# The last batch of a transformer tail in two staggered token halves

## The chip, the cores and the metric

One Trainium2 (trn2) chip; the kernel runs on one of its cores. The metric is device time in microseconds (us) of one execution, median of 3 runs. The core has TensorE (PE, weight loads shown apart as PEld), VectorE (DVE), ScalarE (ACT), GpSimd (POOL) and SyncE (SP), which here issues nearly all DMAs. Each engine has its own instruction stream and works through it in order; engines wait for one another on semaphores.

## The reference

Two layers act on x of 8 batches x 256 tokens x 128 features. Only the end of the second is touched by the change: attention's output product, a linear map with a weight per batch, and a feed-forward part with quantized activations and weights.

```python
def _quant_act(x):
    scale = 127.0 / jnp.clip(jnp.max(jnp.abs(x), axis=-1, keepdims=True), EPS, None)
    xq = jnp.clip(jnp.round(x * scale), -128.0, 127.0) / scale
    return xq                                   # (straight-through terms left out)
def _bitlinear(x, w):
    return jnp.einsum('bsi,oi->bso', _quant_act(x), _quant_weight(w))

x = x + attention(pooled) ...                   # y @ w_out, y: (8, 256, 1024)
c = einsum('bnh,boh->bno', x, weight[subject_id]) + bias[subject_id]
x = x + _bitlinear(gelu(_bitlinear(c, w1)), w2) # 128 -> 512 -> 128
```

## The kernel before

The first 1100 us or so are a state-space layer and a mixture of experts; they are not touched. Then comes attention with the feed-forward part, batch by batch. Four strings of tokens (`ATT_PE`, `ATT_ACT`, `ATT_DVE`, `ATT_GP`) give, for each engine, the order of pieces in one slot; `run` walks through the slots k = -4 to 8 and emits for each token the piece of batch k + shift. The pieces of the end of a batch have the shift -1: they belong to the batch whose heads were done in the slot before. So the end of batch 6 is mixed with the 16 heads of batch 7, while slot 8 holds the end of batch 7 and nothing beside it.

The end of a batch is one chain that passes from engine to engine, for both halves of 128 tokens (t = 0, 1) in one go, all in PSUM bank 7:

- `o2` (PE, L826): y times `Wo`, 16 matmuls over 8 chunks and 2 halves; each f32 matmul is two records in the trace. It waits for the eighth copy of y (`yTe`, ACT, L819).
- `x3` (DVE, L832) adds the residual; `fx` turns it (PE L838, copy ACT L843); `fc` is the product with the batch's weight (PE L849) and the bias (DVE L855).
- `fq` (DVE, L860 to L872): largest magnitude of each token, its scale and inverse, then a multiply and an add of 1.5 * 2^23 per half (L867), which rounds, and two passes that take the constant off, with the bound 127 (L871), and apply the bound -128 (L872), which writes bf16.
- `fqturn` and its copy (PE L886, ACT L891), `fu` (PE L901), gelu (`fg`, ACT L905, two instructions of 128x512); `fq2` is the same quantization on 256x512; `fq2turn` (PE L924), its copy (DVE L929), `fd` (PE L935), `fo` (DVE L943), and one store of 128 KB that SP issues.

`warm:n` (L569) is padding: n products of constants in bank 5, two records each, for the last batch alone. ACT's exp and gelu lie in different tables, and a load stands ahead of the first function of the other set (L905 and L764).

Attention itself: `score` (L747), `tt` (DVE L756), `prob` (exp, ACT L764), `inv` (DVE L770), `norm` (POOL L777, four instructions for a pair of heads), `turn` (PE L785) with a copy on DVE or ACT (L794, L792), `values` (L811), `yturned` (L819).

## Time and profile before

| | us |
|---|---|
| median of 3 runs (lowest, highest) | 1392.04 (1388.57, 1392.33) |
| the profiled execution, its own time | 1390.29 |
| its span, first to last instruction | 1388.5 |
| PE busy, of the span | 1280.7 (92%) |
| DVE / ACT / POOL busy | 1156.7 / 1006.7 / 1106.3 |
| mean granted TensorE clock | 0.985 |
| issue to landing of the eight result stores of 128 KB, lowest / median / highest | 1.8 / 1.9 / 2.7 |

Busy times are sums over stages with different limits. From about 1103 us on, each batch of attention takes 39.86 us; the heads of the last batch end at 1367 us, and what follows is the chain above alone. Starts in the rows are us from the span's start.

### The profile page before, as it was taken

The page shows a single profiled execution, that of the slowest core. Times are in us where ns is not written, and L with a number is a line of the kernel's source. Part 1 is how long each engine was busy: PE and PEld are TensorE (multiplying, and loading weights), DVE is VectorE, ACT ScalarE, POOL GpSimd, SP SyncE. Part 2 cuts the span into 40 slices and gives each one's busy share as a digit, 9 for nine tenths or more (in the row PEclk, how much of TensorE's full clock was granted, in tenths as well). Part 3 has the DMA queues.
Part 4 walks back from the last instruction along what each step waited for, and adds up shares of the span by engine and source line. Part 5 has one row for each costly group of instructions (what it writes and reads, how often), then busy time and mean ns, then how long its engine had stood idle before and what let it go on. Part 6 is the DMA issues. An engine that isn't in the chain of part 4 may idle for free.

```text
span 1388.5 us, 20349 instructions
## 1 busy us (share of the span) xinstructions
PE 1280.7 (92%) x5604; PEld 726.6 (52%) x5613; DVE 1156.7 (83%) x1710; ACT 1006.7 (73%) x2377; POOL 1106.3 (80%) x676
## 2 busy tenths in 40 slices
PE   6598998998998989989989999899999999999997
PEld 2243443343343334334343356689986666766665
DVE  7899999999999999999999989765545466665664
ACT  4778878878878878878878888433326787887783
POOL 7789999999999999999999998034435766856662
PEclk9799999999999999999999999999999999999999
DMA  4645254255164154164244372413221000000000
GB/s 145 274 183 196 109 211 199 106 213 209 65 248 199 70 242 183 69 255 183 108 204 184 130 238 78 145 39 93 80 58 35 9 20 15 22 17 17 9 9 8
DMA packets 48979, 169.29 MB, mean 122 GB/s; under 512 B 15704, under 2 KB 33436, under 8 KB 40716
## 3 DMA queue, kind: packets, MB, share of 16 engines
q1 hardware_dynamic: 46636, 163.78, 30.9%
q0 software_dynamic: 2272, 4.66, 1.5%
q8 instruction: 33, 0.54, 0.2%
q14 instruction: 38, 0.31, 0.1%
HBM read 160.75 MB, written 7.67 MB: 121 GB/s over the span
## 4 chain that ended last, share of the span: by engine, by line
PE 47%; DVE 24%; ACT 14%; issue 11%; DMA 1%; POOL 1%; DVEq 0%; ACTq 0%; POOLq 0%; SPq 0%
DVE h L1255 13%; ACT banks L1220 10%; PE banks L1290 7%; DVE h L1236 5%; PE banks L402 5%; PE banks L747 4%; PE banks L811 3%; PE banks L785 3%; PE banks L411 3%; PE banks L687 2%; PE banks L826 2%; PE banks L704 2%; PE banks L724 2%; PE banks L1141 2%; PE banks L1307 2%
## 5 line engine op out<-in xcount | busy, mean ns | idle before, releaser
L1261 POOL TENSOR_TENSOR h<-h,Cb 128x1024 f32<-128x1024 f32 (+1 forms) x180 | 584.4, 3273 | 24.6 <-DVE h L1255 13.3
L1255 DVE TENSOR_TENSOR_SCAN h<-banks,h 128x1024 f32<-128x1024 f32 x256 | 573.8, 2277 | 15.3 <-ACT banks L1220 14.9
L1220 ACT ACTIVATE banks<-dt,A_cur 128x255 f32<-128x255 f32 x1024 | 422.2, 461 | 86.8 <-DVE h L1255 84.7
L1290 PE MATMUL banks<-h,ident 128*128 128x512 f32 x1024 | 468.8, 597 | 4.4 <-POOL h L1261 2.6
L1290 PEld LDWEIGHTS banks<-h,ident 128*128 128x128 f32 x1024 | 189.9, 190 | 246.5 <-issue 225.3
L1236 DVE TENSOR_TENSOR h<-Bb,banks 128x1024 f32<-128x1024 f32 (+1 forms) x131 | 204.6, 1567 | 3.2 <-ACT banks L1204 3.2
L1242 POOL TENSOR_TENSOR h<-Bb,u 128x1024 f32<-128x1024 f32 x80 | 188.4, 2366 | 0.1
L777 POOL TENSOR_SCALAR h<-h 128x128 f32<-128x128 f32 (+1 forms) x128 | 97.2, 774 | 61.8 <-DVE h L770 61.8
L777 POOL TENSOR_SCALAR Cb<-Cb,h 128x128 f32<-128x128 f32 (+1 forms) x128 | 101.1, 806 | 34.9 <-DVE h L770 34.7
L1115 PE MATMUL banks<-xn,wF 128*128 128x512 f32 x256 | 114.9, 601 | 7.4 <-ACT xn L1107 7.4
L1115 PEld LDWEIGHTS banks<-xn,wF 128*128 128x128 f32 x256 | 48.7, 191 | 72.1 <-issue 61.4
L381 POOL COPY Bb<-Bb 128x1 int32 x39 | 10.5, 268 | 83.2 <-DVE Bb L1663 45.4
L402 PE MATMUL banks<-Cb 128*128 128x128 f32 x624 | 76.1, 275 | 0.2 <-ACT Cb L450 0.2
L402 PEld LDWEIGHTS banks<-Cb 128*128 128x128 f32 x624 | 72.7, 192 | 0.4 <-ACT Cb L450 0.4
L756 DVE CUSTOM_DVE_ANT_0 h<-banks,Bb 128x128 f32<-128x128 f32 (+1 forms) x128 | 38.5, 352 | 26.2 <-PE banks L747 26.1
L747 PE MATMUL banks<-h 64*128 64x128 f32 (+1 forms) x512 | 59.3, 350 | 0.9
L811 PE MATMUL banks<-Bb,h 128*64 128x256 f32 (+1 forms) x512 | 55.7, 338 | 1.3 <-ACT Bb L792 0.8
L487 DVE TENSOR_TENSOR Cb<-Cb,banks 128x512 f32<-128x512 f32 x39 | 26.8, 688 | 36.0 <-PE banks L402 36.0
L764 ACT ACTIVATE Cb<-Cb,h 128x128 f32<-128x128 f32 (+1 forms) x128 | 56.7, 449 | 0.1
L764 ACT ACTIVATE h<-h 128x128 f32<-128x128 f32 (+1 forms) x128 | 56.6, 452 | 0.0
L553 POOL DMA_INDIRECT xm<-by_expert,Bb x32 | 31.5, 985 | 24.1 <-DMA by_expert<-Cb 15.8
L383 POOL DMA_INDIRECT Cb<-by_token,Bb x39 | 38.6, 989 | 14.9 <-POOL Bb L381 14.9
(296 smaller groups left out, 2041.5 us busy)
## 6 DMA issues: line engine op xcount, KB each, us to landing
Bb<-scrX SPq DMA_DIRECT2D x32, 2048.0 KB, 8.0
Cb<-scrX SPq DMA_DIRECT2D x32, 2048.0 KB, 9.5
h<-in_L_ffn_w SPq DMA_DIRECT2D x2, 2048.0 KB, 8.5
by_expert<-Cb SPq DMA_DIRECT2D x39, 64.0 KB, 1.5
h<-in_conv_w SPq DMA_DIRECT2D x4, 512.0 KB, 4.0
scr<-h SPq DMA_DIRECT2D x3, 640.0 KB, 15.0
wF<-scr SPq DMA_DIRECT2D x3, 512.0 KB
dt<-in_pmask SPq DMA_DIRECT2D x4, 257.0 KB, 2.7
```

The lines of the kernel that those rows point to most:

```text
L402: m = e.matmul(bank(2 * w + q)[:, c * P:(c + 1) * P], w_now[q][w][:, c * P:(c + 1) * P], xgT[k], start=True, stop=True)
L747: m = e.matmul(bank(o)[:, lo:lo + n], qT[r:r + HS, p, jc * P:(jc + 1) * P], kT[r:r + HS, p, 0:n], start=True, stop=True)
L764: m = e.activation(Pr[h % 8][:, lo:lo + n], Pr[h % 8][:, lo:lo + n], ACT.Exp, bias=negm[:, jc, h:h + 1], scale=-1.0, accum_out=sums[:, jc, ...
L777: m = e.tensor_scalar(Pr[h % 8][:, lo:lo + n], Pr[h % 8][:, lo:lo + n], inv[:, jc, h:h + 1], None, ALU.mult)
L811: m = e.matmul(bank(4, S)[o * HS:(o + 1) * HS, q0:q0 + n], V[:, kc, h * HS:(h + 1) * HS], PT[h % 4][:, 2 * P * kc:2 * P * kc + n], start=( ...
L1115: m = e.matmul(ps_F[half][:].rearrange("p (b l) -> p b l", b=2), wF[:, FC_TAP + k * 2 * P + half * P:FC_TAP + k * 2 * P + (half + 1) * P], ...
L1220: m = e.activation(ps_dA[c % 2][:, g, half, 1:S], dts[q][:, half, i * S + 1:(i + 1) * S], ACT.Exp, scale=A_cur[q][:, s:s + 1])
L1236: e.tensor_tensor(h[i][:, rows(cs), :, :], both(Bb[i], cs), u_rows(ps_u, cs), ALU.mult).then_inc(sem("mulv"), len(cs))
L1242: e.tensor_tensor(h[i][:, rows(cs), :, :], both(Bb[i], cs), u_rows(us[q][:, :, i * S:(i + 1) * S], cs), ALU.mult).then_inc(sem("mulp"), le ...
L1255: e.tensor_tensor_scan(chunk(i, c), ps_dA_flat[c % 2], chunk(i, c), 0.0, ALU.mult, ALU.add).then_inc(sem("scan"), 1)
L1261: e.tensor_tensor(h[i][:, rows(cs), :, :], h[i][:, rows(cs), :, :], both(Cb[i], cs), ALU.mult).then_inc(sem("hC"), len(cs))
L1290: m = e.matmul(bank(5), ident[:], h_flat[i][:, s * HALVES * S:(s + 1) * HALVES * S], start=(s == 0), stop=(s == NS - 1))
```

## The change

All pieces of slot 8 with the shift -1 leave the common loop. For the last batch their place is taken by new functions that treat one half of the tokens each, in an order of their own (`ENDING`). Half 0 works in bank 7, half 1 in bank 6, each with its own semaphore steps. The copy before `fd` moves from DVE to ACT. `gelus` loads the gelu table right behind the last copy of y. The result is stored in two DMAs of 64 KB.

In every batch, `q_clip` loses its second instruction: the first writes bf16 directly, with the bound 127 and no bound at -128 (the scale makes no value go below -127).

In slot 8 of the loop `warm:l8` and `warm:l23` are gone; `warm:l2` stays in `ATT_PE` (its piece has the shift 0, so it isn't skipped), and `ENDING` has `warm:2`, `warm:8` and `warm:5`.

```diff
@@ -367,8 +367,11 @@
                     mask(b + 3)
                 if b + 1 < B:
                     conditioned(b + 1)
-                result(b)
-            e.wait_ge(sem("out"), 16 * B + 16)
+                    result(b)
+            for t in range(2):
+                e.wait_ge(sem("f_o"), 2 * B + 1 + t)
+                dma(out_tok[:, END * 2 + t:END * 2 + t + 1, :], fo[:, t:t + 1, :], "out")
+            e.wait_ge(sem("out"), 16 * B + 32)
 
 
         def tail_gpsimd(e):
@@ -868,12 +871,11 @@
 
         def q_clip(m, tmp_t, dst, name):
             m.sync()
-            m(m.e.tensor_scalar(tmp_t, tmp_t, -ROUND, 127.0, ALU.add, ALU.min)); m.sync()
-            m.e.tensor_scalar(dst, tmp_t, -128.0, None, ALU.max).then_inc(sem(name), 1)
+            m.e.tensor_scalar(dst, tmp_t, -ROUND, 127.0, ALU.add, ALU.min).then_inc(sem(name), 1)
 
         def dve_fq(e, b):
             e.wait_ge(sem("f_c"), b + 1)
-            m = Chain(e, "du", chained[0] + b * 14)
+            m = Chain(e, "du", chained[0] + b * 12)
             q_scales(m, fc, 1)
             q_round(m, fc, ft)
             q_clip(m, ft, fq, "f_q")
@@ -906,7 +908,7 @@
 
         def dve_fq2(e, b, step):
             e.wait_ge(sem("f_g"), 2 * b + 2)
-            m = Chain(e, "du", chained[0] + b * 14 + 7)
+            m = Chain(e, "du", chained[0] + b * 12 + 6)
             if step == 0:
                 q_scales(m, fg, 0)
             elif step == 1:
@@ -944,6 +946,105 @@
                                        scalar=fr[:, 0, t:t + 1], in1=fst[:, t, :], op0=ALU.mult, op1=ALU.add
                                        ).then_inc(sem("f_o"), 1)
 
+
+        def half(x, t):
+            return x[:, t * P:(t + 1) * P]
+
+        def pe_o2_end(e, part):
+            t = 1 if part else 0
+            e.wait_ge(sem("yTe"), 8 * B)
+            e.wait_ge(sem("f_o"), 2 * B)
+            for c in ((range(8), range(4), range(4, 8))[part]):
+                m = e.matmul(bank(7 - t, P), yT[:, c, t * P:(t + 1) * P], Wo[:, c, :], start=(c == 0), stop=(c == 7))
+            if part != 1:
+                m.then_inc(sem("o2"), 1)
+
+        def dve_x3_end(e, t):
+            e.wait_ge(sem("o2"), B + t)
+            e.tensor_tensor(fst[:, t, :], xt[:, 2 * END + t, :], bank(7 - t, P), ALU.add).then_inc(sem("x3"), 1)
+
+        def pe_fx_end(e, t):
+            e.wait_ge(sem("x3"), B + t)
+            e.transpose(bank(7 - t, P), fst[:, t, :], ident[:]).then_inc(sem("fx_ps"), 1)
+
+        def act_fx_end(e, t):
+            e.wait_ge(sem("fx_ps"), B + t)
+            e.activation(half(fx3T, t), bank(7 - t, P), ACT.Copy).then_inc(sem("fx"), 1)
+
+        def pe_fc_end(e, t):
+            e.wait_ge(sem("fx"), B + t)
+            e.wait_ge(sem("cw"), 32 * B)
+            e.matmul(bank(7 - t, P), half(fx3T, t), fcw, start=True, stop=True).then_inc(sem("fc_ps"), 1)
+
+        def dve_fc_end(e, t):
+            e.wait_ge(sem("fc_ps"), B + t)
+            e.wait_ge(sem("cw"), 32 * B)
+            e.tensor_tensor(fc[:, t, :], bank(7 - t, P), fcb, ALU.add).then_inc(sem("f_c"), 1)
+
+        def levels_end(m, t, src, dst, row, tmp_t, name):
+            m(m.e.tensor_reduce(fr[:, 2, t:t + 1], src[:, t, :], AX_X, ALU.max, apply_absolute_value=True)); m.sync()
+            m(m.e.tensor_scalar(fr[:, 2, t:t + 1], fr[:, 2, t:t + 1], Q_EPS, 1.0 / 127.0, ALU.max, ALU.mult)); m.sync()
+            m(m.e.reciprocal(fr[:, 3, t:t + 1], fr[:, 2, t:t + 1]))
+            m(m.e.tensor_scalar(fr[:, row, t:t + 1], fr[:, 2, t:t + 1], fsm[:, 10 + (row != 1):11 + (row != 1)], None,
+                                ALU.mult)); m.sync()
+            m(m.e.tensor_scalar(tmp_t[:, t, :], src[:, t, :], fr[:, 3, t:t + 1], ROUND, ALU.mult, ALU.add)); m.sync()
+            m.e.tensor_scalar(dst[:, t, :], tmp_t[:, t, :], -ROUND, 127.0, ALU.add, ALU.min).then_inc(sem(name), 1)
+
+        def dve_fq_end(e, t):
+            e.wait_ge(sem("f_c"), B + t)
+            levels_end(Chain(e, "du", chained[0] + END * 12 + t * 5), t, fc, fq, 1, ft, "f_q")
+
+        def pe_fqturn_end(e, t):
+            e.wait_ge(sem("f_q"), B + t)
+            e.transpose(half(bank(7 - t).bitcast(BF16), 0), fq[:, t, :], idb).then_inc(sem("fqT_ps"), 1)
+
+        def act_fqturned_end(e, t):
+            e.wait_ge(sem("fqT_ps"), B + t)
+            e.activation(half(fqT, t), half(bank(7 - t).bitcast(BF16), 0), ACT.Copy).then_inc(sem("fqT"), 1)
+
+        def pe_fu_end(e, t):
+            e.wait_ge(sem("fqT"), B + t)
+            e.matmul(bank(7 - t), half(fqT, t), f1q, start=True, stop=True).then_inc(sem("fu_ps"), 1)
+
+        def act_gelus_end(e):
+            e.preload_act_table_set("gelu_and_others")
+
+        def act_fg_end(e, t):
+            act_fg(e, END, t)
+
+        def dve_fq2_end(e, t):
+            e.wait_ge(sem("f_g"), 2 * B - 1 + t)
+            levels_end(Chain(e, "du", chained[0] + END * 12 + 10 + t * 5), t, fg, fq2, 0, ft2, "f_q2")
+
...
+        def dve_fo_end(e, t):
+            e.wait_ge(sem("fd_ps"), B + t)
+            e.wait_ge(sem("out"), 16 * B)
+            e.scalar_tensor_tensor(out=fo[:, t, :], in0=bank(7 - t, P), scalar=fr[:, 0, t:t + 1], in1=fst[:, t, :],
+                                   op0=ALU.mult, op1=ALU.add).then_inc(sem("f_o"), 1)
+
+        ENDS = dict(
+            gp=dict(),
+            pe=dict(warm=lambda e, n: turn_over(e, 5, n), o2=pe_o2_end, fx=pe_fx_end,
+                    fc=pe_fc_end, fqturn=pe_fqturn_end, fu=pe_fu_end, fq2turn=pe_fq2turn_end, fd=pe_fd_end),
+            act=dict(fx=act_fx_end, fqturned=act_fqturned_end, fg=act_fg_end, fq2turned=act_fq2turned_end),
+            dve=dict(x3=dve_x3_end, fc=dve_fc_end, fq=dve_fq_end, fq2=dve_fq2_end, fo=dve_fo_end))
 
         PIECES = dict(
             gp=dict(gather=(4, gp_gather), norm=(0, gp_norm)),
@@ -964,11 +1065,19 @@
                 for token in order.split():
                     name, _, arg = token.partition(":")
                     shift, fn = PIECES[engine][name]
+                    if k == B and shift < 0:
+                        continue
                     shift += {"l": -1, "n": 1}.get(arg[:1], 0)
                     if not isinstance(k, int) or 0 <= k + shift < B:
                         fn(e, k + shift, *((int(arg.lstrip("ln")),) if arg else ()))
             for k in range(-4, B + 1):
                 slot(k)
+            for token in ENDING[engine].split():
+                name, _, arg = token.partition(":")
+                if name == "gelus":
+                    act_gelus_end(e)
+                else:
+                    ENDS[engine][name](e, int(arg))
 
 
         block = ctx.enter_context(nc.Block())
@@ -1944,12 +2053,19 @@
 
 
 X2T_AFTER = (3, 4, 5)
+END = B - 1
+ENDING = dict(
+    gp="",
+    pe="""o2:0 o2:1 fx:0 o2:2 fc:0 fx:1 fc:1 warm:2 fqturn:0 fu:0 fqturn:1 fu:1 warm:8
+       fq2turn:0 fd:0 warm:5 fq2turn:1 fd:1""",
+    act="gelus fx:0 fx:1 fqturned:0 fg:0 fqturned:1 fg:1 fq2turned:0 fq2turned:1",
+    dve="x3:0 x3:1 fc:0 fq:0 fc:1 fq:1 fq2:0 fq2:1 fo:0 fo:1")
...
 ATT_PE = """
 score:4 turn:2 o2 hold:12 pturn score:5 turn:3 values:0 fx turn:4 warm:l2 pool score:6 fc turn:5 values:1 turn:6 q:0
-score:7 turn:7 k:0 values:2 warm:l8 turn:8 turn:9 fqturn q:1 fu:0 score:n0 values:3 fu:1 k:1 turn:10 turn:11 fold
-heat:32 x2t q:2 warm:5 turn:12 score:n1 values:4 q:3 k:2 at warm:l23 turn:13 score:n2 values:5 v:0 fq2turn k:3 S
+score:7 turn:7 k:0 values:2 turn:8 turn:9 fqturn q:1 fu:0 score:n0 values:3 fu:1 k:1 turn:10 turn:11 fold
+heat:32 x2t q:2 warm:5 turn:12 score:n1 values:4 q:3 k:2 at turn:13 score:n2 values:5 v:0 fq2turn k:3 S
...
```

PE, from the padding ahead of the output product to the turn of the quantized values. Before (L826 output product, L838 `fx`, L849 `fc`, L569 padding, L886 `fqturn`):

```order
L569 MATMUL banks<-ident,center_w 128x128 x3
L826 MATMUL banks<-h,Cb 128x128 x16
L838 MATMUL banks<-ident,yz 128x128 x2
L569 MATMUL banks<-ident,center_w 128x128 x2
L849 MATMUL banks<-xs,u 128x128 x2
L569 MATMUL banks<-ident,center_w 128x128 x8
L886 MATMUL banks<-Bb,dt 128x128 x2
```

The same place now (L958 output product, L968 `fx`, L977 `fc`, L572 padding, L999 `fqturn`):

```order
L572 MATMUL banks<-ident,center_w 128x128 x5
L958 MATMUL banks<-h,Cb 128x128 x12
L968 MATMUL banks<-ident,yz 128x128
L958 MATMUL banks<-h,Cb 128x128 x4
L977 MATMUL banks<-xs,u 128x128
L968 MATMUL banks<-ident,yz 128x128
L977 MATMUL banks<-xs,u 128x128
L572 MATMUL banks<-ident,center_w 128x128 x2
L999 MATMUL banks<-Bb,dt 128x128
```

The turn of half 0 has moved in between the chunks of half 1, and the two padding products that stood behind `fx` now stand with the other three ahead of the output product.

PE, from `fu` to its last instruction. Before (L901 `fu`, L924 `fq2turn`, L935 `fd`):

```order
L901 MATMUL banks<-xs,dt 128x512 x2
L569 MATMUL banks<-ident,center_w 128x128 x23
L924 MATMUL banks<-Bb,h 128x128 x8
L935 MATMUL banks<-xs,Bb 128x128 x8
L88 UNCONDITIONAL_BRANCH
```

Now (L1007 `fu`, L1022 `fq2turn`, L1033 `fd`):

```order
L1007 MATMUL banks<-xs,dt 128x512
L999 MATMUL banks<-Bb,dt 128x128
L1007 MATMUL banks<-xs,dt 128x512
L572 MATMUL banks<-ident,center_w 128x128 x8
L1022 MATMUL banks<-Bb,h 128x128 x4
L1033 MATMUL banks<-xs,Bb 128x128 x4
L572 MATMUL banks<-ident,center_w 128x128 x5
L1022 MATMUL banks<-Bb,h 128x128 x4
L1033 MATMUL banks<-xs,Bb 128x128 x4
```

The padding is in two lots, and each lot stands ahead of the turn of one half.

ACT, from the last two copies of y to its end. Before (L819 copy of y, L843 `fx`, L891 `fqturned`, L905 gelu):

```order
L819 ACTIVATE Cb<-banks 128x256 x2
L843 ACTIVATE u<-banks 128x256
L891 ACTIVATE dt<-banks 128x256
L905 ACT_TABLE_LOAD
L905 ACTIVATE h<-banks,yz 128x512 x2
```

Now (L822 copy of y, L972 `fx`, L1003 `fqturned`, L907 gelu, L1027 the copy ahead of `fd`):

```order
L822 ACTIVATE Cb<-banks 128x256 x2
L1010 ACT_TABLE_LOAD
L972 ACTIVATE u<-banks 128x128 x2
L1003 ACTIVATE dt<-banks 128x128
L907 ACTIVATE h<-banks,yz 128x512
L1003 ACTIVATE dt<-banks 128x128
L907 ACTIVATE h<-banks,yz 128x512
L1027 ACTIVATE Bb<-banks 128x512 x2
```

The load has moved ahead of both `fx` copies, and ACT has two more instructions of 128x512. On DVE the new order is `x3:0 x3:1`, then bias and quantization of half 0, the same of half 1, then both of the second quantization, then `fo:0 fo:1`.

## Rows read from the trace of the kernel before

**Rows 1.** Busy time by window, one steady batch: us, busy us (instructions), clock, DMA share, GB/s.

```profile
1222.54:1262.40 39.86, 39.61 (x289) 27.41 (x290) 26.00 (x116) 31.86 (x104) 24.96 (x33) 1.00 0.05 14
```

**Rows 2.** The chain that ended last, in the last heads: start, us, what.

```profile
1358.53 1.48 issue
...
1361.48 2.39 POOL Cb L777 x3
```

**Rows 3.** Timeline from 1366 us on: start, us, engine line op, xcount, idle before.

```profile
1366.63 0.94 PE L569 MATMUL banks<-ident,center_w 128*128 128x128 f32 x6
...
1367.40 3.74 PE L826 MATMUL banks<-h,Cb 128*128 128x128 f32 x32
...
1372.56 0.71 PE L849 MATMUL banks<-xs,u 128*128 128x128 f32 x4
...
1374.23 0.17 DVE L861 TENSOR_SCALAR yz<-yz 128x2 f32<-128x2 f32 x1
...
1374.76 0.48 DVE L867 TENSOR_SCALAR dt<-u,yz 128x128 f32<-128x128 f32 x2
...
1376.28 0.38 ACT L891 ACTIVATE dt<-banks 128x256 bf16<-128x256 bf16 x1 [3.76 <-PE banks L886]
1376.68 1.28 ACT L905 ACT_TABLE_LOAD   x1
...
1376.94 0.38 PE L901 MATMUL banks<-xs,dt 128*128 128x512 bf16 x1 [0.70 <-ACT dt L891]
...
1383.52 0.62 PE L924 MATMUL banks<-Bb,h 128*128 128x128 bf16 x8 [1.07 <-DVE h L872]
...
1385.59 0.61 DVE L943 SCALAR_TENSOR_TENSOR Bb<-banks,yz 128x128 f32<-128x128 f32 x2 [0.71 <-PE banks L935]
```

**Rows 4.** DVE groups by shape, 1371 to 1389 us: xcount, busy us, mean ns, idle before.

```profile
L860 DVE TENSOR_REDUCE yz<-h 128x2 f32<-128x1024 f32 x1 | 1.2, 1220 | 3.4 <-ACT h L905 3.4
L867 DVE TENSOR_SCALAR h<-h,yz 128x512 f32<-128x512 f32 x2 | 0.9, 483 | 0.0
L872 DVE TENSOR_SCALAR h<-h 128x1024 bf16<-128x1024 f32 x1 | 0.7, 695 | 0.0
...
L943 DVE SCALAR_TENSOR_TENSOR Bb<-banks,yz 128x128 f32<-128x128 f32 x2 | 0.6, 348 | 0.7 <-PE banks L935 0.7
...
L855 DVE TENSOR_TENSOR u<-banks,xs 128x256 f32<-128x256 f32 x1 | 0.4, 425 | 1.7 <-PE banks L849 1.7
...
L860 DVE TENSOR_REDUCE yz<-u 128x2 f32<-128x256 f32 x1 | 0.4, 420 | 0.0
...
L872 DVE TENSOR_SCALAR dt<-dt 128x256 bf16<-128x256 f32 x1 | 0.3, 294 | 0.0
```

**Rows 5.** ACT groups by shape, 900 to 1389 us.

```profile
L455 ACT ACTIVATE Cb<-banks 128x512 f32<-128x512 f32 x39 | 23.3, 597 | 23.8 <-PE banks L402 23.8
...
L450 ACT ACTIVATE Cb<-banks 128x128 f32<-128x128 f32 x39 | 10.7, 278 | 54.1 <-PE banks L394 54.1
...
L905 ACT ACTIVATE h<-banks,yz 128x512 f32<-128x512 f32 x16 | 10.1, 684 | 0.1
```

**Rows 6.** DVE's timeline at 1360 us.

```profile
1360.59 0.74 DVE L872 TENSOR_SCALAR h<-h 128x1024 bf16<-128x1024 f32 x1
```

**Rows 7.** POOL groups: first instruction of the last `norm`; two like it, 1355.5 to 1358.6 us.

```profile
L777 POOL TENSOR_SCALAR Cb<-Cb,h 128x128 f32<-128x128 f32 x1 | 1.4, 1421 | 1.5 <-DVE h L770 1.5
...
L777 POOL TENSOR_SCALAR Cb<-Cb,h 128x128 f32<-128x128 f32 x2 | 1.2, 602 | 0.0
```

**Rows 8.** Windows in the state-space layer and in the old tail, columns as in rows 1.

```profile
160.00:162.00 2.00, 0.05 (x2) 0.03 (x1) 2.00 (x3) 1.97 (x4) 2.00 (x2) 1.00 0.45 188
162.00:163.00 1.00, 1.00 (x2) 0.48 (x3) 0.93 (x1) 1.00 (x4) 1.00 (x1) 0.55 0.00 0
...
1374.00:1377.00 3.00, 1.41 (x13) 1.21 (x13) 1.72 (x8) 0.71 (x2) 0.00 (x0) 1.00 0.00 0
```

**Rows 9.** PE groups, 907 to 911 us, where the granted clock was 0.50.

```profile
L569 PE MATMUL banks<-ident,center_w 128*128 128x128 f32 x10 | 2.3, 421 | 0.0
```

More of the change, by code:

```diff
@@ new lines, in pe_fq2turn_end, with act_fq2turned_end, pe_fd_end @@
+        def pe_fq2turn_end(e, t):
+            e.wait_ge(sem("f_q2"), B + t)
+            for c in range(FC):
+                m = e.transpose(half(bank(7 - t).bitcast(BF16), c), fq2[:, t, c * P:(c + 1) * P], idb)
+            m.then_inc(sem("fq2T_ps"), 1)
+        def act_fq2turned_end(e, t):
+            e.wait_ge(sem("fq2T_ps"), B + t)
+            e.activation(fq2T[:, t, :, :], fold(bank(7 - t).bitcast(BF16)[:, 0:FC * P], FC), ACT.Copy
+                         ).then_inc(sem("fq2T"), 1)
+        def pe_fd_end(e, t):
+            e.wait_ge(sem("fq2T"), B + t)
+            for c in range(FC):
+                m = e.matmul(bank(7 - t, P), fq2T[:, t, c, :], f2q[:, c, :], start=(c == 0), stop=(c == 3))
+            m.then_inc(sem("fd_ps"), 1)
```

## The prediction

> **What bounds the kernel now.** I first read the busy windows of the attention stage. A steady batch takes 39.86 us, and PE is busy for 39.61 of them, DVE for 26.00 and ACT for 31.86 [rows 1]: seven of the eight batches are bound by PE. The reader is to see there that a DVE instruction less per batch can give at most the 0.25 us in which PE isn't busy. The chain of waits then shows where this ends: in the heads of the last batch it runs through POOL's `norm`, and there is a wait of 1.48 us in it, in which POOL stands until ACT has done the last exps [rows 2]. Last comes the timeline behind the last `values`. From 1367.40 us, when the output product starts, to 1386.20, when the second `fo` is done, every step waits for the one before it [rows 3]: 18.80 us, on engines of which one works at a time. The store and its end take the 2.29 us up to the span's end. The change works on these 18.80 us, so durations and hand-overs count here, and no engine's share does.
>
> **Output product to `fc`.** I count from the start of the output product as 0. Its 32 records take 3.74 us, 0.112 us from start to start [rows 3]. Half 0 is done after 16 of them, at 1.96; the addition takes 0.29 (425 ns for 256 elements less 128 times 1.04 ns, the slope between the two reductions of 420 and 1220 ns) [rows 4]. `x3:0` is thus done at 2.29, `fx:0` fits in between the chunks of half 1 (it delays them by 0.14), and its copy on ACT takes 278 ns [rows 5]. The product ends at 3.88, `x3:1` at 4.21, and `fc:0` on PE at 4.16, with the 0.3 us of a single f32 product there [rows 3]. From here DVE has no pause: it is what sets the end of the first quantization.
>
> **First quantization.** One half: reduction 0.29, the three operations on the scales 0.53 from the start of L861 to that of L867 [rows 3], L867 0.28 (483 ns less 384 times 0.52), and the one pass that is left 0.23 (294 ns less 128 times 0.52 ns, where 0.52 is the slope up to 695 ns) [rows 4]; with hand-overs of 0.04 this is 1.41 us. With the bias before it (0.29 and 0.04) half 0 is done at 5.97 and half 1 at 7.73. Before, the turned values of both halves were ready for ACT 8.88 after the start (L891 at 1376.28 [rows 3]); those of half 1 now are at 8.05, after a turn of 0.22. So the second set of small operations has eaten most of what the stagger gives here: 0.83 us are left.
>
> **The way through PE and ACT.** From 5.97 on half 0 goes on beside DVE's work for half 1: turn 0.22 and 0.06 to get there, copy 0.28, `fu` 0.38, gelu 0.68 (684 ns, [rows 5]), 1.77 with the hand-overs, so the gelu is done at 7.74, when DVE is free too. This needs the table to be there. Before, ACT's load ran from 1376.68 to 1377.96, and `fu` was done by about 1377.15, so the load cost 0.8 us of waiting [rows 3]. Now it runs while PE computes the output product, which takes 3.74 us against 1.28 for the load; nothing else is asked of ACT there. If that cover were gone, the 0.6 us that the load would overhang come back.
>
> [...]
>
> **Second quantization.** One half of 512 elements: 0.69 for the reduction, 0.53, L867 0.48, last pass 0.43 [rows 4], 2.20 with hand-overs. DVE does both without a pause: 9.98 and 12.21. Before, PE got the result at 16.12 (L924 at 1383.52 [rows 3]). This step carries most of the gain: 0.8 from the table, 0.7 from the pass that is dropped, and the rest from half 0's way through PE and ACT, which is hidden now.
>
> **The end, and the padding.** `fu:1` is issued at 8.6. Behind it stand 16 records of padding, 1.8 us, up to 10.40; `fq2turn:0` was ready at 10.04 and waits. It takes 0.39 for 4 of the 8 products of 0.62 [rows 3], the copy on ACT 0.60 (597 ns, [rows 5]; before it was on DVE, 0.69 for both halves), `fd:0` 0.39: done at 11.88. Then 10 records of padding hold PE up to 12.84, while half 1 is ready for it at 12.27. So here the change adds a wait of 0.57 us, with `fq2turn:1`, `fd:1`, DVE's `fo:1` and SP's second store queued behind it. Turn 0.39, copy 0.60, `fd:1` 0.39, `fo:1` 0.35 and four hand-overs give 14.70. Against 18.80 this is 4.10 us less. SP has no other transfer by then, and the first store (ready at 12.6) is 2 us ahead. The second is 64 KB instead of 128 KB; its price isn't in the trace. A store of 128 KB took 1.8 to 2.7 us to land, so it lies between 0.9 lost (median to highest) and 0.4 gained (if half the moving goes); I take 0.15 gained, since nothing but size differs from the median one.
>
> **Ahead of the output product.** The padding there was 6 records and is 10 now, since `warm:l2` runs one place earlier than it did. The product started right behind the padding (6 records from 1366.63 on, then 1367.40 [rows 3]), so 4 x 0.112 = 0.45 us are lost. In the last heads L872 goes away beside the last `norm`. POOL's first instruction there took 1421 ns, from 1360.06 to 1361.48 [rows 7], where the same shape took 602 in the `norm` before it, and DVE's L872 stood from 1360.59 to 1361.33 beside it [rows 6]. The 0.82 us extra lie beside 0.50 us of L871 and 0.74 us of L872; by its share L872's part is 0.5. The path from there to the output product is POOL, turn, `values`, and moves up with it. [...] The two other effects of the dropped pass come to nothing: the first quantization of batch 6, which stands ahead of an `inv` of the last heads, lets POOL start 0.3 earlier, but that runs into the wait of 1.48 [rows 2]; in the seven PE-bound batches I take 0, bounds 0 and 7 x 0.25 = 1.75.
>
> [...]
>
> **Sum.** 4.10 + 0.15 - 0.45 + 0.50 = 4.3 us. The profiled execution took 1390.29, hence 1386.0. The median of the three runs shown is 1.75 above it, the lowest 1.72 below; the mean of all four times is 1390.8. A median of the changed kernel is as likely to lie high as low, so I forecast 1386.5.
>
> **Rivals.** *Padding at half clock.* The new order leaves PE with little to do from 5.8 to 8.5: two turns and two products, with pauses of up to 1.1 us. [...] In the old tail it held 1.00 through 3 us in which PE was busy for 1.41 [rows 8]; the new pauses have about as much work between them. If it falls, the padding costs twice as much, 0.23 us a record instead of 0.112 (10 took 2.3 us at half clock [rows 9]): the first lot ends at 12.2, the second at 16.2, `fo:1` at 18.35. Of the 4.3 us 3.65 are gone: 1389.6 against the profiled execution.
>
> *The PE-bound batches gain too.* If PE's 0.25 us are waits for DVE, the seven batches give up to 1.75 more: 1384.2. For it: PE's weight loads for L811 sometimes wait for a DVE copy. Against: the matmuls before them are still running then.
>
> *A collision in each batch, the side of slower.* With L872 gone DVE reaches its next passes 0.74 us earlier, and they may fall beside a `norm` that had been free; one costs POOL 0.82 us as above. If PE waited for it in each of the seven batches, 5.7 us come on top: 1391.7, slower than before. It decides from the sixth batch that pays. Against it: POOL is idle for 14.9 of 39.86 us, and PE isn't waiting for it [rows 1].
>
> **Chances.** The sum 60%, the PE-bound batches 15%, the half clock 18%, the collisions 7%. A measurement of this kernel tells about 0.3%, 4.2 us, from no change, and the sum lies right at that line: of its 60 I give 38 to faster and 22 to within. With 15 for the PE-bound batches faster has 53; within has 22, 16 of the half clock and 5 of the collisions, 43; slower by over 0.3% is left with 4. The range takes in the half clock below and the gain in the batches above: 1383.2 to 1390.0.
>
> **What would show it.** Right: one table load between the last copy of y and `fx:0`; DVE without a pause from `x3:1` to the end of the second quantization, some 8.3 us; `fo:1` 14.7 us after the start of the output product; PE's padding right up to `fq2turn:1`; 10 records of padding ahead of the product; the last `norm` in about 3.3 us instead of 3.80; steady batches of 39.86. Wrong: a granted clock under 1.00 between `fqturn:0` and `fd:1`; steady batches shorter or longer by over 0.1 us; DVE pauses of over 0.2 us ahead of `fq2:0`, which would mean that half 0's way through PE and ACT is longer than the 1.77 us.

## The result and the profile after

The changed kernel takes 1385.96 us (median of 8, 1385.39 to 1390.67) where the kernel before takes 1390.15 in the same comparison (median of 8, 1388.57 to 1392.33): ratio 0.9973, 95% interval 0.9961 to 0.9985. By the medians that is 4.2 us faster, 0.5 us under the forecast of 1386.5; by the ratio it is 3.8 us, with an interval from 2.1 to 5.4. The interval leaves out a ratio of 1, so the kernel is faster; but 0.27% is a little under the 0.3% that the prediction took as the least that can be told from no change. Its profiled execution took 1387.39 us, with a span of 1385.6 and a mean granted clock of 0.986.

That execution is only 2.9 us under the profiled one of before. The first record of the first output product in the attention stage shows why. It is at 1102.79 us before:

```profile
1102.79 0.61 PE L826 MATMUL banks<-h,Cb 128*128 128x128 f32 x4
```

and at 1104.60 after:

```profile
1104.60 0.61 PE L829 MATMUL banks<-h,Cb 128*128 128x128 f32 x4
```

All that comes ahead of it is state-space work that the change doesn't touch, and it took 1.81 us longer in this execution. In the traces of e1 to e4 below, which ran on one chip, this start lies between 1101.30 and 1104.32, so it moves by some 3 us from one execution to the next. I therefore measure each trace from this record on, in three distances: *heads*, up to the start of the last output product; *ending*, from there to the end of the last `fo`; *store*, from there to the end of the span (the span is given to 0.1 us, so this last one is good to 0.05).

| us | before | after | difference | predicted |
|---|---|---|---|---|
| heads | 264.61 | 264.60 | -0.01 | -0.05 (0.45 lost, 0.50 gained) |
| ending | 18.80 | 14.41 | -4.39 | -4.10 |
| store | 2.30 | 1.99 | -0.31 | -0.15 |
| together | 285.71 | 281.00 | -4.71 | -4.3 |

The steady batch, the window that answers to [rows 1] (columns as there):

```profile
1224.35:1264.21 39.86, 39.60 (x289) 27.41 (x290) 25.09 (x114) 31.84 (x104) 24.52 (x33) 1.00 0.05 14
```

DVE has 0.91 us less to do, the batch is as long as it was. The ending, the timeline that answers to [rows 3]; the output product starts at 1369.20:

```profile
1367.98 1.38 PE L572 MATMUL banks<-ident,center_w 128*128 128x128 f32 x10
...
1368.49 1.28 ACT L1010 ACT_TABLE_LOAD   x1
1369.20 2.84 PE L958 MATMUL banks<-h,Cb 128*128 128x128 f32 x24
1371.19 0.29 DVE L964 TENSOR_TENSOR yz<-Cb,banks 128x128 f32<-128x128 f32 x1 [3.38 <-PE banks L958]
...
1374.77 0.23 DVE L991 TENSOR_SCALAR dt<-dt 128x128 bf16<-128x128 f32 x1
1374.92 0.28 DVE L982 TENSOR_TENSOR u<-banks,xs 128x128 f32<-128x128 f32 x1
...
1375.65 0.10 PEld L1007 LDWEIGHTS banks<-xs,dt 128*128 128x128 bf16 x1 [0.50 <-ACT dt L1003]
...
1376.09 0.69 ACT L907 ACTIVATE h<-banks,yz 128x512 f32<-128x512 f32 x1 [0.48 <-remote]
1376.37 0.23 DVE L991 TENSOR_SCALAR dt<-dt 128x128 bf16<-128x128 f32 x1
...
1376.81 0.69 DVE L985 TENSOR_REDUCE yz<-h 128x1 f32<-128x512 f32 x1 [0.21 <-ACT h L907]
...
1377.48 1.95 PE L572 MATMUL banks<-ident,center_w 128*128 128x128 f32 x16
...
1379.27 0.39 PE L1022 MATMUL banks<-Bb,h 128*128 128x128 bf16 x4
...
1380.58 1.33 PE L572 MATMUL banks<-ident,center_w 128*128 128x128 f32 x10
1380.62 0.43 DVE L991 TENSOR_SCALAR h<-h 128x512 bf16<-128x512 f32 x1
...
1381.75 0.39 PE L1022 MATMUL banks<-Bb,h 128*128 128x128 bf16 x4
1382.17 0.60 ACT L1027 ACTIVATE Bb<-banks 128x512 bf16<-128x512 bf16 x1 [1.88 <-PE banks L1022]
1382.82 0.40 PE L1033 MATMUL banks<-xs,Bb 128*128 128x128 bf16 x4 [0.69 <-ACT Bb L1027]
1383.26 0.35 DVE L1039 SCALAR_TENSOR_TENSOR Bb<-banks,yz 128x128 f32<-128x128 f32 x1 [1.95 <-PE banks L1033]
```

The reader is to see three things. The table load lies beside padding and output product. From 1373.08 (`x3:1`) to 1381.05 DVE stops once, for 0.21 us. And `fq2turn:1` (L1022, the second time) has its input at 1381.05 and its first product at 1381.75, because padding is ahead of it. One record is missing: the product of `fu:0` (L1007), of which only the weight load at 1375.65 was recorded, so the gelu behind it shows "remote" as its releaser. POOL's first instruction of the last `norm`, the group that answers to [rows 7]:

```profile
L780 POOL TENSOR_SCALAR Cb<-Cb,h 128x128 f32<-128x128 f32 x1 | 1.0, 972 | 1.9 <-DVE h L773 1.9
```

972 ns instead of 1421. Windows (columns as in rows 1) of the long pause of PE in the last heads, and of the thin and the full stretch of the ending:

```profile
1359.90:1362.30 2.40, 0.01 (x2) 0.00 (x0) 1.72 (x6) 2.29 (x10) 0.54 (x2) 1.00 0.00 0
1362.30:1366.00 3.70, 2.95 (x27) 2.03 (x29) 1.68 (x4) 1.03 (x3) 2.90 (x4) 1.00 0.00 0
1374.00:1377.00 3.00, 1.40 (x8) 1.03 (x9) 2.52 (x13) 1.11 (x4) 0.00 (x0) 1.00 0.00 0
1377.00:1379.00 2.00, 1.75 (x15) 1.72 (x16) 1.86 (x7) 0.89 (x2) 0.00 (x0) 1.00 0.00 0
```

The granted clock is 1.00 in all of them. In the third window PE was busy for more than the 1.40 us shown, since the missing `fu:0` lies in it; e11 below has its record, 0.39 us, which makes 1.79. The experiments show that in both places the clock is less certain than it looks.

### The profile page after: what moved, and what is told of

Read it like the earlier page. It is cut to its first block, busy times and chain, and to the rows that moved or that the text cites. A ratio compares the mean times of both kernels' runs of the same rounds, so it can differ in the third digit from the quotient of the medians.

```text
span 1385.6 us, 20287 instructions
## 1 busy us (share of the span) xinstructions
PE 1276.5 (92%) x5572; PEld 722.1 (52%) x5581; DVE 1150.2 (83%) x1705; ACT 1008.1 (73%) x2381; POOL 1102.0 (80%) x676
## 4 chain that ended last, share of the span: by engine, by line
PE 47%; DVE 23%; ACT 14%; issue 11%; DMA 2%; POOL 1%; DVEq 0%; ACTq 0%; SPq 0%; POOLq 0%
DVE h L1364 13%; ACT banks L1329 10%; PE banks L1399 7%; DVE h L1345 5%; PE banks L405 5%; PE banks L750 4%; PE banks L814 3%; PE banks L788 3%; PE banks L414 3%; PE banks L690 2%; PE banks L707 2%; PE banks L727 2%; PE banks L1416 2%; PE banks L1250 2%; PE banks L829 2%
## 5 line engine op out<-in xcount | busy, mean ns | idle before, releaser
L780 POOL TENSOR_SCALAR Cb<-Cb,h 128x128 f32<-128x128 f32 (+1 forms) x128 | 98.0, 782 | 37.1 <-DVE h L773 37.0
L453 ACT ACTIVATE Cb<-banks 128x128 f32<-128x128 f32 x39 | 10.8, 277 | 54.8 <-PE banks L397 54.8
```

The lines of the kernel that those rows point to most:

```text
L780: m = e.tensor_scalar(Pr[h % 8][:, lo:lo + n], Pr[h % 8][:, lo:lo + n], inv[:, jc, h:h + 1], None, ALU.mult)
```

## The experiments

Ratios are against the kernel before, run in the same comparison. e1 to e4 ran on one chip, e5 to e8 on a second and e9 to e12 on a third (the kernel before took 1390.51, 1406.11 and 1405.66 us there). The distances are of each one's trace. A steady batch takes 39.86 us on all three chips, so the distances can be compared; medians can't, ratios with care.

| us | heads | ending | store | median | ratio (95%) |
|---|---|---|---|---|---|
| before | 264.61 | 18.80 | 2.30 | 1390.15 | |
| after | 264.60 | 14.41 | 1.99 | 1385.96 | 0.9973 (0.9961 to 0.9985) |
| e1 one-pass rounding alone | 264.66 | 17.73 | 2.29 | 1390.41 | 0.9996 (0.9987 to 1.0005) |
| e2 two-pass rounding | 265.03 | 16.26 | 2.01 | 1388.16 | 0.9981 (0.9972 to 0.9990) |
| e3 no early load | 264.62 | 16.58 | 2.00 | 1387.72 | 0.9978 (0.9969 to 0.9987) |
| e4 halves in step | 264.58 | 20.54 | 1.93 | 1392.29 | 1.0016 (1.0006 to 1.0025) |
| e5 no padding in the ending | 265.21 | 14.20 | 2.03 | 1401.14 | 0.9965 (0.9953 to 0.9978) |
| e6 lots 2 and 3 doubled | 264.60 | 17.31 | 1.96 | 1404.38 | 0.9985 (0.9975 to 0.9994) |
| e7 no `warm:l2` | 264.14 | 14.41 | 1.99 | 1400.50 | 0.9961 (0.9949 to 0.9974) |
| e8 one store | 265.22 | 14.41 | 2.31 | 1401.85 | 0.9966 (0.9955 to 0.9978) |
| e9 as e3, pauses filled | 264.60 | 15.01 | 2.02 | one run | |
| e10 as e2, pauses filled | 265.05 | 14.96 | 2.00 | one run | |
| e11 leaner ending | 264.76 | 13.61 | 2.02 | 1399.39 | 0.9948 (0.9928 to 0.9968) |
| e12 as e11, last heads padded | 264.14 | 13.60 | 2.00 | 1399.91 | 0.9956 (0.9939 to 0.9973) |

Among the 17 executions of the kernel before that stand beside e9 to e12, one took 3347.41 us and is in no ratio, and one took 1416.12 us at a mean clock of 0.934 and is in them. The ratio of e11 is lower than its medians give (1399.39 to 1405.66, 0.9955).

**e1, the rounding alone.** The kernel before with

```diff
-            m(m.e.tensor_scalar(tmp_t, tmp_t, -ROUND, 127.0, ALU.add, ALU.min)); m.sync()
-            m.e.tensor_scalar(dst, tmp_t, -128.0, None, ALU.max).then_inc(sem(name), 1)
+            m.e.tensor_scalar(dst, tmp_t, -ROUND, 127.0, ALU.add, ALU.min).then_inc(sem(name), 1)
```

> The kernel before with the one-pass rounding alone (last batch in its old form, old padding). My theory: PE bounds the steady batches, so they stay at 39.86 us; the last norm on POOL falls from 3.80 to about 3.3 us; in the last batch the two dropped passes take 0.29 and 0.70 us off the 18.80 us from the start of the last output product to the second fo, which comes to 17.8. In all about -1.5 us. Rival (PE waits for DVE in the batches): the batches come to 39.6 and the time falls by up to 1.75 more, -3.2. Rival (collisions with POOL): batches longer than 39.96 and a time above the kernel before.

Measured: batches of 39.86 us, last `norm` 3.35 us, ending 17.73. The ending and the batches came as expected, and both rivals fall. The 0.45 us of the `norm` don't show in the heads, though (264.66 and not 264.15), and the timed runs show 0.1 us, within an interval from 1.8 us faster to 0.7 slower. In this trace the kernel gained 1.0 us from the first output product on, where 1.5 was expected. What took the 0.5 back is told below e8.

**e2, two passes again in the changed kernel.** The edit above undone, and in the ending

```diff
-            m.e.tensor_scalar(dst[:, t, :], tmp_t[:, t, :], -ROUND, 127.0, ALU.add, ALU.min).then_inc(sem(name), 1)
+            m(m.e.tensor_scalar(tmp_t[:, t, :], tmp_t[:, t, :], -ROUND, 127.0, ALU.add, ALU.min)); m.sync()
+            m.e.tensor_scalar(dst[:, t, :], tmp_t[:, t, :], -128.0, None, ALU.max).then_inc(sem(name), 1)
```

> The changed kernel with the rounding in two passes again, in the batches and in both halves of the ending. My theory: DVE sets the end through both quantizations, and per half a second pass costs about 0.23 + 0.04 us (first) and 0.43 + 0.04 us (second), so four of them lengthen the ending's 14.41 us by 1.5 to 15.9, less what the padding held anyway (0.65 us ahead of fq2turn:1: PE's padding would be done before DVE, so only about 0.9 to 1.0 net, 15.3 to 15.4). The last norm goes back to about 3.80. In all +1.4 us. Rival (the clip is hidden, hand-overs set the ending): the ending stays under 14.8.

The `norm` is back at 3.80 and the heads are 0.43 longer, as expected. The ending is longer than expected by 0.9 us, 16.26. Windows of this trace (columns as in rows 1), and the second lot of padding in its timeline:

```profile
1372.00:1375.00 3.00, 1.13 (x6) 0.38 (x5) 2.72 (x12) 1.24 (x3) 0.00 (x0) 1.00 0.00 0
1376.00:1378.00 2.00, 2.00 (x11) 1.94 (x10) 1.86 (x7) 0.02 (x1) 0.00 (x0) 0.50 0.00 0
```

```profile
1375.14 3.07 PE L572 MATMUL banks<-ident,center_w 128*128 128x128 f32 x16
```

The clock has fallen to 0.50 after a stretch in which PE was busy for 1.13 of 3 us, and the 16 records take 3.07 instead of 1.95 us.

**e3, no early load.**

```diff
-    act="gelus fx:0 fx:1 fqturned:0 fg:0 fqturned:1 fg:1 fq2turned:0 fq2turned:1",
+    act="fx:0 fx:1 fqturned:0 fg:0 fqturned:1 fg:1 fq2turned:0 fq2turned:1",
```

> The changed kernel without the early load of the gelu table: the load of 1.28 us then stands between the copy fqturned:0 and gelu 0. My theory: the copy ends 6.4 us after the start of the output product, fu:0 at 6.7 hides 0.3 of it, the load ends at about 7.7 and gelu 0 at 8.4 instead of 7.58; DVE pauses for about 1.0 us ahead of fq2:0 instead of 0.2, and the padding's 0.65 us of hold takes the rest: fo:1 at about 14.6 to 14.7. Copies behind the load (fqturned:1) wait too, so gelu 1 comes at about 9.1, which DVE does not need before 10.4. In all +0.2 to +0.8. [...]

The ending is 16.58, over the expected 14.7. The timeline of this trace shows what the load took:

```profile
1373.44 0.28 ACT L1003 ACTIVATE dt<-banks 128x128 bf16<-128x128 bf16 x1 [1.26 <-PE banks L999]
...
1373.74 1.28 ACT L907 ACT_TABLE_LOAD   x1
...
1375.03 0.69 ACT L907 ACTIVATE h<-banks,yz 128x512 f32<-128x512 f32 x1
...
1375.76 0.69 DVE L985 TENSOR_REDUCE yz<-h 128x1 f32<-128x512 f32 x1 [1.03 <-ACT h L907]
...
1376.17 3.35 PE L572 MATMUL banks<-ident,center_w 128*128 128x128 f32 x16
```

The load takes 1.28 us; it starts 0.02 us behind the copy, the gelu starts 0.01 us behind the load, and it is done at 8.40 us from the start of the output product, as expected. The rest is the clock again, 0.50 from 1377 to 1379.

**e4, the halves in step.** The waits of half 0 are raised to both halves, nothing else:

```diff
         def pe_fqturn_end(e, t):
-            e.wait_ge(sem("f_q"), B + t)
+            e.wait_ge(sem("f_q"), B + 1)
         def pe_fq2turn_end(e, t):
-            e.wait_ge(sem("f_q2"), B + t)
+            e.wait_ge(sem("f_q2"), B + 1)
         def dve_fq2_end(e, t):
-            e.wait_ge(sem("f_g"), 2 * B - 1 + t)
+            e.wait_ge(sem("f_g"), 2 * B)
```

> The changed kernel with the two halves in step instead of staggered: fqturn and fq2turn of half 0 wait for the quantization of both halves, fq2 of half 0 for both gelus. All instructions are the same. My theory: the stagger hides half 0's way through PE and ACT beside DVE's work. fqturn:0 then starts at 7.4 instead of 5.9, the gelus are done at about 9.2 and 9.9 and the second quantization starts at 9.9 instead of 7.6: 2.3 us later; it ends at 14.2; both halves are then turned, copied and multiplied one behind the other, fo:1 at about 17.2 to 17.7, 2.8 to 3.3 us later than the 14.41. Rival (small halves and not the overlap give the gain): fo:1 under 15.5.

The ending is 20.54, 6.13 us longer, and the kernel is slower than the one before. The second quantization ends at 14.90 instead of 11.85, which is 3.05 later (expected: 2.3). The timeline shows the 0.75 that were not expected, and the larger part of the other 3.1 us:

```profile
1376.31 0.69 ACT L907 ACTIVATE h<-banks,yz 128x512 f32<-128x512 f32 x1 [0.48 <-PE banks L1007]
...
1376.89 0.27 ACT L1003 ACTIVATE dt<-banks 128x128 bf16<-128x128 bf16 x1
...
1384.10 2.36 PE L572 MATMUL banks<-ident,center_w 128*128 128x128 f32 x10
...
1386.26 0.63 PE L1022 MATMUL banks<-Bb,h 128*128 128x128 bf16 x4
```

In ACT's order `fqturned:1` stands behind `fg:0`. Its input was there at 1376.33, but it started at 1376.89, beside the end of the gelu; so the second gelu was done at 10.6 instead of the expected 9.9, and DVE waits for both. And I had overlooked that the third lot of padding stands between `fd:0` and `fq2turn:1`: in step both halves are ready ahead of it, and it took all of its time, at half clock (0.55 from 1384 to 1386), 2.2 us up to the turn of half 1.

So e4 measures more than the overlap. Less those 2.2 us the ending would be about 18.4 us (an estimate), about 4.0 over the staggered one, of which 0.75 are ACT's order. That is still more than the 17.73 of e1, which has whole halves and the same rounding. Halves alone gain nothing; the overlap carries the change.

**e5, no padding in the ending.**

```diff
-    ... fc:1 warm:2 fqturn:0 fu:0 fqturn:1 fu:1 warm:8 fq2turn:0 fd:0 warm:5 fq2turn:1 fd:1
+    ... fc:1 fqturn:0 fu:0 fqturn:1 fu:1 fq2turn:0 fd:0 fq2turn:1 fd:1
```

> The changed kernel without the three lots of padding products in the ending (2, 8 and 5). My theory: the second lot of 16 records does not hold fq2turn:0 much, the third of 10 holds fq2turn:1 by 0.65 us, so fo:1 comes 0.65 us earlier, at 13.75 after the start of the output product, if the granted clock stays at 1.00. Rival (the padding keeps the clock): it falls below 1.00 between fu:1 and fd:1, the eight products of fd:1 and the turns cost twice as much (0.6 us more) and fo:1 comes at 14.3 or later.

14.20, between the two. The clock did fall, and it stayed down to the last product:

```profile
1392.00:1394.00 2.00, 0.62 (x2) 0.19 (x2) 1.66 (x7) 1.36 (x3) 0.00 (x0) 1.00 0.00 0
1395.00:1399.00 4.00, 2.33 (x16) 1.27 (x15) 2.13 (x8) 1.19 (x2) 0.00 (x0) 0.50 0.06 16
```

The turn and `fd` of half 1 took 0.61 us each instead of 0.39 and 0.40, 0.43 together; of the 0.65 us that PE isn't held any more, 0.22 are left, and 0.21 were measured.

**e6, more padding.** `warm:8` to `warm:16`, `warm:5` to `warm:10`.

> The changed kernel with the second lot of padding doubled (16 turn-overs, 32 records) and the third too (10, 20 records). A record takes 0.112 us. My theory: PE is held by what is queued ahead: the second lot ends 1.79 us later, at 12.0 instead of 10.2 after the start of the output product, fq2turn:0 (ready at 10.0) waits for it, then fd:0 and 2.24 us of padding up to about 15.8, then 1.85 us to fo:1, 17.6 to 17.8: 3.3 us later. The rival (padding of no price, since PE is idle there) says 14.4.

17.31, 2.90 later, with the clock at 1.00: a little under my 17.6, and the rival falls. PE's padding is on the path here, where it is longer than its pause.

**e7, without `warm:l2` in `ATT_PE`.**

> The changed kernel without the 4 padding records ahead of the output product that were moved there (in the batches before they go as well, for the last batch alone they are issued). My theory: PE goes from the last values through 6 instead of 10 records, and the last output product starts 0.45 us earlier, from first to last output product 264.0 us instead of 264.44. Rival (yTe, the last copy of y, is what the product waits for): no difference, 264.44.

264.14 instead of 264.60: the four records cost 0.46 us.

**e8, one store.** `result(END)` in place of the two DMAs.

> The changed kernel with one store of 128 KB after both fo instead of two of 64 KB. My theory: only the size of the last store matters; from the end of fo:1 to the end of the span 1.99 us with two stores, 2.29 with one (the value of the kernel before), +0.3. Rival (two stores cost the queue a second issue and the number of stores matters, not their size): the same or shorter than 1.99.

2.31 instead of 1.99: the size of the last store counts, 0.32 us for 64 KB.

*The heads of e1, e5 and e8.* They are 0.5 to 0.6 us longer than those of kernels with the same heads (e7 for e1, the changed kernel for e5 and e8). Windows of e8 (columns as in rows 1), at the pause that PE makes there:

```profile
1374.00:1376.00 2.00, 0.11 (x1) 0.14 (x2) 1.36 (x5) 1.75 (x8) 0.59 (x1) 1.00 0.00 0
1376.00:1379.00 3.00, 3.00 (x21) 2.06 (x21) 0.43 (x2) 0.88 (x2) 2.77 (x4) 0.54 0.00 0
```

The clock fell behind the pause; in e6 and e7, with the same pause and the same work, it stayed at 1.00. So it differs between executions of the same instructions. But the kernel has a part in it too: the pause ends with the turn of head 13, and the timelines of the kernel before and of the changed one show it longer now:

```profile
1360.54 0.52 PE L785 MATMUL banks<-ident,Cb 128*128 128x128 f32 x3 [2.08 <-ACT Bb L792]
```

```profile
1362.33 0.52 PE L788 MATMUL banks<-ident,Cb 128*128 128x128 f32 x3 [2.42 <-ACT Bb L795]
```

The pause is 2.07 or 2.08 us in the three traces with two passes (before, e2, e10) and 2.40 to 2.42 in the ten that have one pass and leave the pause unfilled. The clock fell in four of these ten (e1, e5, e8 and e11 below) and in none of the three. That is too few to tell whether the longer pause brings the fall, or whether it happens to the kernel before as well.

**e9 and e10, price of load and rounding without that of the clock.** e3 and e2 with padding in PE's pauses, e9:

```diff
-    ... fqturn:0 fu:0 fqturn:1 fu:1 warm:8 ...
+    ... fqturn:0 warm:1 fu:0 warm:2 fqturn:1 warm:4 fu:1 warm:8 ...
```

and e10 in the same way with `warm:1`, `warm:3`, `warm:1`.

> The changed kernel without the early table load, with padding products in PE's pauses (2 records ahead of fu:0, 4 ahead of fqturn:1, 8 ahead of fu:1), so that the granted clock stays at 1.00. It separates the price of the load from that of the clock, which fell in e3 (0.73 in 1376 to 1377 us, then 0.50, 16 records of padding in 3.35 us instead of 1.95; tail 16.58 us). My theory: e3's +2.17 us are about 0.95 of load (gelu 0 is done 0.8 us later, then a PE that is still held by its third lot of padding) and 1.2 of half clock. Tail here 15.2 to 15.5 us, granted clock 1.00 throughout. Rival: the load costs it all and the clock nothing, tail 16.5.

> The changed kernel with the rounding in two passes, and padding in PE's pauses (2 records ahead of fu:0, 6 ahead of fqturn:1, 2 ahead of fu:1). The clock fell in e2 too (0.87 in 1375 to 1376 us, then 0.50; tail 16.26 us). My theory: with the clock at 1.00 DVE is the bound, done with fq2:1 13.05 us after the start of the output product as in e2, and PE is there at once: fo:1 at 15.0 instead of 14.41, so four passes are worth only about 0.6 net in the ending, and the other 1.25 us of e2 are the clock. Rival: DVE alone explains e2, tail 16.2 again.

e9 ends at 15.01, a little under the expected 15.2, and e10 at 14.96, as expected; the clock is at 1.00 throughout both endings. The window of e9 in which e3 had lost its clock, and the same padding:

```profile
1389.00:1392.00 3.00, 2.83 (x24) 2.57 (x24) 1.83 (x7) 2.02 (x4) 0.00 (x0) 1.00 0.00 0
```

```profile
1390.62 1.95 PE L572 MATMUL banks<-ident,center_w 128*128 128x128 f32 x16
```

So the early load is worth 0.60 us, the one-pass rounding 0.55, and half the clock cost 1.57 us in e3 (16.58 less 15.01) and 1.30 in e2 (16.26 less 14.96), more than what was tested in either. The load would have cost more but for the padding: the first gelu is done 0.83 us later in e9 than in the changed kernel, where the second lot had held `fq2turn:0` for 0.24. Filling the pauses cost nothing that shows; in e9 `fu:0` and `fu:1` start 0.05 and 0.06 us behind their copies.

All this rests on one trace of each kernel. By the ratios e2 is only 0.0008 (1.1 us) and e3 0.0005 (0.7 us) behind the changed kernel, where the traces say 2.3 and 2.2; the intervals are too wide to decide. Whether the clock falls in every execution of e2 and e3, or only in some as in the last heads, is not shown.

**e11 and e12, a version from the findings.** No `warm:l2`, no third lot, the last copy on DVE; e12 has `warm:9` ahead of `turn:13` in `ATT_PE` as well.

```diff
-       fq2turn:0 fd:0 warm:5 fq2turn:1 fd:1""",
-    act="gelus fx:0 fx:1 fqturned:0 fg:0 fqturned:1 fg:1 fq2turned:0 fq2turned:1",
-    dve="x3:0 x3:1 fc:0 fq:0 fc:1 fq:1 fq2:0 fq2:1 fo:0 fo:1")
+       fq2turn:0 fd:0 fq2turn:1 fd:1""",
+    act="gelus fx:0 fx:1 fqturned:0 fg:0 fqturned:1 fg:1 fq2turned:0",
+    dve="x3:0 x3:1 fc:0 fq:0 fc:1 fq:1 fq2:0 fq2:1 fo:0 fq2turned:1 fo:1")
```

> The changed kernel without the 4 padding records ahead of the output product, without the third lot of padding (10 records between fd:0 and fq2turn:1), and with the last copy of turned values on DVE, which is idle by then, instead of ACT; the first two lots of padding stay. My theory: the first two lots keep the clock at 1.00 through the ending (as in the changed kernel), the 0.65 us of hold go, and the DVE copy of 512 elements takes about 0.4 us instead of 0.60. From first to last output product 264.14 (264.75 where the clock falls in the last heads), tail 13.5 to 13.6 instead of 14.41. In all -1.3 us against the changed kernel, -5.5 against the kernel before, 0.9960. Rival (the clock falls after the second lot as it did in e5): tail 14.0 or more.

> The kernel of e11 with 18 more records of padding in PE's pause of 2.4 us in the last heads (between the values of heads 8 and 9 and the turn of head 13, at 1359.9 to 1362.3 us in the changed kernel). In e1, e5 and e8 the granted clock fell to 0.50 there for about 3 us, in the others not, and where it fell the last output product came 0.5 to 0.6 us later. My theory: with the pause filled (2.0 us of 2.4) the clock stays at 1.00 there in every execution, from first to last output product 264.14; the median moves by at most 0.3 us against e11, since only a part of the executions had the fall. Rival: the padding holds the turn of head 13, which is on the path of the last heads, and the distance grows to 264.5 or more.

Both end in 13.6 us, with the copy on DVE in 0.43 (e12's timeline):

```profile
1394.30 0.40 PE L1022 MATMUL banks<-Bb,h 128*128 128x128 bf16 x4 [0.36 <-DVE h L991]
...
1394.73 0.43 DVE L1032 COPY Bb<-banks 128x512 bf16<-128x512 bf16 x1 [0.23 <-PE banks L1022]
...
1395.65 0.35 DVE L1043 SCALAR_TENSOR_TENSOR Bb<-banks,yz 128x128 f32<-128x128 f32 x1 [0.49 <-PE banks L1037]
```

In the last heads of e11 the clock fell, in those of e12, with their pause filled, it stayed, and the output product started 0.62 us earlier. First e11, then e12:

```profile
1376.00:1380.00 4.00, 3.87 (x25) 2.92 (x25) 1.41 (x4) 0.87 (x2) 3.00 (x4) 0.57 0.00 0
```

```profile
1374.00:1380.00 6.00, 5.08 (x49) 3.88 (x48) 2.98 (x7) 3.20 (x11) 3.35 (x4) 1.00 0.01 3
```

e12 takes 279.74 us from the first output product to the end of the span, against 281.00 for the changed kernel and 285.71 for the one before: the expected 1.3 us. The timed runs show both faster than the kernel before; between e11, e12 and the changed kernel the intervals overlap, so that these 1.3 us, and whatever the padded heads give, rest on the traces alone; and as the clock stayed up there in six of ten traces without that padding, one trace doesn't show that it was the padding that kept it.

## Why the prediction held, step by step

**What bounds it.** Right. The batches stayed at 39.86 us in every trace, with one pass or two, and the 4.71 us came from the ending, as [rows 3] had said.

**Output product to `fc`, first quantization.** `x3:0` started at 1.99 (said: 1.96), half 0's levels were done at 5.80 (5.97), half 1's at 7.40 (7.73). I had put a hand-over of 0.04 us behind each last pass; in the trace the next operation starts 0.08 us before the pass ends (1374.77 and 0.23 to 1374.92).

**The way through PE and ACT.** 1.78 us (said: 1.77). But since half 1's levels came 0.33 earlier and this way didn't, DVE now waits for the gelu, 0.21 us. The prediction had named a pause of over 0.2 as a sign of a longer way; it was a sign of faster levels. The table load was hidden; its worth, 0.60, is 0.2 under my 0.8, which was for the old order. That it equals the 0.6 that I gave for a missing cover is luck: the gelu came 0.83 later, and the padding took 0.24 of that. The load follows the copy at once, 0.02 us behind it here and in e3, 0.01 in e9, and takes 1.28 us in each. Nor is there a wait behind it: in e3 the load ends at 1375.02, and the gelu starts at 1375.03.

**The end and the padding.** The second quantization was done at 11.85 (12.21), PE was held for about 0.65 us (0.57), `fo:1` was done at 14.41 (14.70). The gain of 4.39 is the predicted 4.10 and these 0.29. I had split it in part by the old order, with 0.7 for the dropped pass of the second quantization; in the new order both passes together give 0.55 (e10), since PE's padding takes back what DVE saves on half 1. Taken out one at a time, the load is worth 0.60, the rounding 0.55 and the overlap about 4.0; against them stand the small operations done twice and 0.80 us that e11 gets back from the third lot and the last copy on ACT.

**The store.** 0.31 gained, confirmed by e8. I had taken 0.15, with bounds of 0.4 gained and 0.9 lost; from the median to the highest landing it is 0.8 (1.9 to 2.7).

**Ahead of the output product.** 0.46 lost (said: 0.45; e7), 0.45 gained in the `norm` (said: 0.5; the heads of e2 are 0.43 longer). POOL's first instruction was still 0.37 us over its 602 ns, beside 0.50 us of DVE's single pass. Before, it was 0.82 over, beside 0.50 of L871 and 0.74 of L872. My 0.5 was an estimate that split the 0.82 by these shares; it leaves 0.33 for one pass of 0.50, and 0.37 were measured. In both traces the instruction is longer where DVE's passes lie beside it; what lengthens it isn't shown. The other effect, on the `inv` of the last heads, came to nothing as said: POOL's wait ahead of this `norm` grew from 1.5 to 1.9 us, and the `norm` started no earlier.

**The rival of the half clock.** It named the right danger, and its price was wrong. The changed kernel keeps the clock through its ending in its own trace and in those of e6, e7 and e8. In e2 to e5, with less work or longer pauses there, it fell, but each of them has a single trace. The price was 1.3 to 1.6 us and not 3.65, because the clock was back for the third lot in e2 and e3 (10 records in 1.33 us); I had let it stay at half to the end. What the prediction missed is the pause in the last heads: a fall there cost 0.5 to 0.6 us in four traces, and the dropped pass made that pause 0.34 us longer.

**The other rivals.** Neither was seen: no batch gained, none had a collision.

**What was luck.** The trace says 4.71 us and the sum said 4.3, by terms that each came out within 0.3 us. That the median lies within 0.5 us of 1386.5 says less: the part ahead of the change moves by 3 us from one execution to the next, and the 1386.5 had in it a mean of four times of the kernel before.

**What stays open.** Why the state-space part differs by up to 3 us between executions of the same code. One of the eight timed runs of the changed kernel took 1390.67 us at a mean clock of 0.979, where the other seven have 0.984 to 0.987; that a fall of the clock did this wasn't shown, as it has no trace.

## What to carry to other kernels

Where every step waits for the one before, two staggered halves gain by what lies beside each other (here: one half's way through PE and ACT beside DVE's work), and not by being small; in step they gained nothing. Every such change makes PE's pauses longer or shorter somewhere, so read the granted clock at each pause again, and judge an edit of a few tenths only once the pauses are filled: the traces of e2 and e3 alone would have made the rounding and the load look worth over three times what they are. Padding belongs in pauses that are longer than itself, never right ahead of a step that is about to be ready. When the work ahead of a change varies by more than the change brings, measure distances inside the traces from a mark behind that work.

## What the runs showed of the hardware

- The clock fell to 0.50 behind stretches in which PE was busy for 1.13 of 3 us (e2) or 0.62 of 2 (e5), and held behind 1.79 of 3 (the changed kernel, with the record that is missing). Behind a pause of 2.4 us without work in the last heads it held in some executions and fell in others, with the same instructions. So these stretches are examples and no limit.
- With full padding behind it a fall was short: in e3 the clock was at 0.50 from 1377 us and back at 1.00 from 1380 on. In e5, without padding, it was at 0.50 from 1395 to 1399 us and not back before the last product.
- Two stores of 64 KB ended 0.32 us sooner than one of 128 KB (the changed kernel and e8), with the first issued over 2 us ahead of the second.
- DVE copied 128x512 bf16 elements out of PSUM in 0.43 us (e12), ACT in 0.60 (the changed kernel).
